# Three float32r products for the last four down projections of a dense FFN

## The reference, cut to what matters

```python
h = silu(x @ w_gate) * (x @ w_up)                 # 1024 tokens x 1024
a = abs(h.reshape(B, S, I // 4, 4))
_, idx = top_k(a, 2)                              # the two largest of each four stay
h_sparse = (g * mask).reshape(B, S, I)
return h_sparse @ w_down                          # 1024 x 256
...
x = x + tanh(g_ffn[1]) * ffn(layernorm(x))
```

## Time and profile before

| what | value |
|---|---|
| device time, 3 runs | 359.84 us median, 358.69 to 361.1 |
| profiled execution: its device time | 358.81 us |
| its span, and mean granted PE clock | 357.1 us, 0.976 |
| PE busy | 318.0 us (89%) |
| DVE busy | 258.3 us (72%) |
| ACT busy | 162.8 us (46%) |
| POOL busy | 110.3 us (31%) |

### The profile page before, as it was taken

The page is one execution under the profiler, slowest core; times in us unless marked ns, Lnnn a source line. Parts: engine busy times, 40 slices in busy tenths (PEclk is TensorE's granted clock), DMA queues, the critical chain, the costliest instruction groups (busy, mean ns, idle before and its releaser), DMA issues.

```text
span 357.1 us, 5054 instructions
## 1 busy us (share of the span) xinstructions
PE 318.0 (89%) x1630; PEld 218.0 (61%) x1639; DVE 258.3 (72%) x572; ACT 162.8 (46%) x333; POOL 110.3 (31%) x156
## 2 busy tenths in 40 slices
PE   2799886669999987999989999998979999999997
PEld 1385676547899634555544554563444886788885
DVE  4538895776677649989967996895672479999921
ACT  2333455344444222147767766775784344333000
POOL 7503575272000275501443425243554001000000
PEclk9999999658999999999999999999999999999999
DMA  6999200025311224600000000000000000000101
GB/s 190 369 418 323 51 1 16 2 88 180 101 61 59 76 59 130 284 0 9 0 7 2 1 0 9 0 3 1 6 3 0 0 2 0 2 0 0 46 30 44
DMA packets 14090, 22.96 MB, mean 64 GB/s; under 512 B 2065, under 2 KB 11409, under 8 KB 13202
## 3 DMA queue, kind: packets, MB, share of 16 engines
q1 hardware_dynamic: 13298, 20.56, 16.8%
q0 software_dynamic: 768, 2.10, 1.9%
HBM read 16.36 MB, written 6.03 MB: 63 GB/s over the span
## 4 chain that ended last, share of the span: by engine, by line
PE 61%; DVE 21%; issue 5%; ACT 4%; DMA 4%; POOL 4%; SPq 1%; DVEq 0%; ACTq 0%; POOLq 0%
PE bank L272 44%; DVE mx L1332 6%; PE bank L492 5%; PE bank L460 4%; ACT region L1008 3%; DVE stats L1078 2%; PE bank L463 2%; DMA region<-y_sorted,place 2%; PE bank L288 2%; POOL rstd L774 2%; DVE x_sb L1118 1%; DVE xn L1090 1%; PE bank L282 1%; PE bank L507 1%; POOL region L814 1%
## 5 line engine op out<-in xcount | busy, mean ns | idle before, releaser
L1008 ACT ACTIVATE region<-bank,padcol 128x512 f32<-128x512 f32 x96 | 62.3, 692 | 18.6 <-PE bank L272 17.8
L1332 DVE TENSOR_REDUCE mx<-bank 128x2 f32<-128x512 f32 (+1 forms) x96 | 60.9, 681 | 4.7 <-PE bank L463 4.1
L841 POOL TENSOR_SCALAR_AFFINE_SELECT region<-region 128x1024 f32<-128x1024 f32 x32 | 35.8, 1121 | 77.8 <-ACT region L1008 77.8
L272 PE MATMUL bank<-qst,kblk 128*128 128x512 f32 x96 | 45.7, 488 | 0.8 <-DMA qst<-nmT 0.3
L460 PE MATMUL bank<-kblk,qst 128*128 128x512 f32 x96 | 43.6, 471 | 1.7 <-DVE mx L1332 1.3
L463 PE MATMUL bank<-causb,identb 128*128 128x256 bf16 (+1 forms) x90 | 28.3, 314 | 0.0
L272 PE MATMUL bank<-e_down,region 128*128 128x256 f32 x128 | 28.0, 380 | 0.0
L1118 DVE SCALAR_TENSOR_TENSOR x_sb<-bank,tg,x_sb 128x256 f32<-128x256 f32 x24 | 11.6, 483 | 21.0 <-PE bank L272 21.0
L272 PEld LDWEIGHTS bank<-e_down,region 128*128 128x128 f32 x128 | 24.2, 190 | 3.6 <-DVE region L1481 0.3
L774 POOL TENSOR_TENSOR rstd<-veps,power 128x1 f32<-128x1 f32 x40 | 24.8, 619 | 3.3
L770 POOL TENSOR_SCALAR veps<-mv 128x1 f32<-128x1 f32 x40 | 12.8, 321 | 40.3 <-DVE mv L1080 37.5
(11 more groups left out here) (195 smaller groups left out, 737.0 us busy)
## 6 DMA issues: line engine op xcount, KB each, us to landing
e_gu<-in_e_gu_dram SPq DMA_DIRECT2D x2, 1408.0 KB, 12.2
x_sorted<-zero SPq DMA_DIRECT2D x1, 1920.0 KB, 9.4
y_sorted<-region SPq DMA_DIRECT2D x15, 128.0 KB, 1.7
x_sb<-in_x_dram SPq DMA_DIRECT2D x4, 256.0 KB, 4.1
ctxT<-in_ctxT_dram SPq DMA_DIRECT2D x2, 512.0 KB, 7.3
e_down<-in_e_down_dram SPq DMA_DIRECT2D x1, 1024.0 KB, 13.6
region<-x_sorted SPq DMA_DIRECT2D x1, 1024.0 KB, 7.4
e_gu<-in_f_gate_dram SPq DMA_DIRECT2D x1, 1024.0 KB, 6.5
```

The source lines that it names most:

```text
L272: return pe.matmul(dst, lhsT, rhs, start=first, stop=last)
L841: pool.affine_select(out=block, in_=block, compare_op=ALU.is_ge, fill=0.0, base=0, pattern=[[0, 2], [0, PER_GROUP], [1, P]], channel_multi ...
L1008: taken(act.activation(dst, src.rearrange("p (h n) -> p h n", n=SEQ - mt * P), ACT.Exp, bias=padcol[:, key:key + 1], scale=float(HD) ** -0 ...
L1332: taken(dve.reduce_max(mx[:, b % 2, nt, quads, q, hg], src, AX), "sa")
```

## The change

Four new tiles are laid over storage that is free by then: `fd_high` (in `qst`, behind the comparison results), `fd_low` (over `vaug`), `h_high` (over `kblk`) and `h_low` (over `hs[1]` itself). ACT rounds `f_down` into `fd_high` in two halves of 128x1024, behind the silu of pieces 0 and 1. POOL subtracts the two halves into `fd_low`, behind its last `inverse_std` in program order. At the end of its program ACT rounds the eight finished blocks of `hs[1]` into `h_high`, each as soon as DVE has written it, and DVE subtracts them in place into `h_low`, behind the last choice and the residual of tile 3. PE makes tiles 4 to 7 in two passes: for all four tiles the two products with `h_high` (64 matmuls), then for all four the product with `h_low` (32 matmuls). Two pairs of semaphores of earlier stages are merged into one each (`a_abs` into `a_made`, `tanh` and `vexp` into `tanh_vexp`), with the counts of their waits adapted; the order of instructions there stays.

```diff
--- before.py
+++ after.py
@@ -187,6 +187,10 @@
                   "fu": ([up_high[t][:, :] for t in range(KT)], up_low, f_up)}
 
         cmps = sb_over("cmps", [P, 6, UNIT], BF16, "qst")
+        fd_high = sb_over("fd_high", [P, FFN_MT, DIM], F32R, "qst", 2 * 6 * UNIT)
+        fd_low = sb_over("fd_low", [P, FFN_MT, DIM], F32R, "vaug")
+        h_high = sb_over("h_high", [P, FFN_MT, UNIT], F32R, "kblk")
+        h_low = sb_over("h_low", [P, FFN_MT, UNIT], F32R, "region", 4 * 6144)
         cmp1, cmp2, cmp3 = cmps[:, 0:3, :], cmps[:, 3:5, :], cmps[:, 5, :]
         wins = amat[:, :, :].rearrange("p h n -> p (h n)").bitcast(BF16).rearrange("p (c n) -> p c n", n=UNIT)
 
@@ -335,7 +339,7 @@
                 if i == 2:
                     gate(0)
                 dst = acquire(pe, "ro", i, "main")
-                pe.wait_ge(sem("a_made"), 2 * h + 2)
+                pe.wait_ge(sem("a_made"), 4 * h + 4)
                 for t in range(2):
                     ins = mm(dst, amat[:, h, t * SEQ + st * P:t * SEQ + st * P + P], v0[:, t, h, :], t == 0, t == 1)
                 ready(ins, "ro")
@@ -682,9 +686,20 @@
             pe.wait_ge(sem("hs_made"), 8)
             for k in range(UNIT_TILES):
                 down(k, "last")
-            pe.wait_ge(sem("hs_made"), 16)
+            pe.wait_ge(sem("fd_split"), 4)
             for k in range(UNIT_TILES, TILES):
-                down(k, "wide")
+                dst = acquire(pe, "res3", k, "wide")[:, 0:DIM]
+                cols = tile_cols(k % UNIT_TILES)
+                for m in range(FFN_MT):
+                    pe.wait_ge(sem("ffn_high"), 2 + m + 1)
+                    mm(dst, h_high[:, m, cols], fd_high[:, m, :], m == 0, False)
+                    mm(dst, h_high[:, m, cols], fd_low[:, m, :], False, False)
+            for k in range(UNIT_TILES, TILES):
+                cols = tile_cols(k % UNIT_TILES)
+                for m in range(FFN_MT):
+                    pe.wait_ge(sem("h_low"), m + 1)
+                    ins = mm(fills["res3", k][:, 0:DIM], h_low[:, m, cols], fd_high[:, m, :], False, m == FFN_MT - 1)
+                ready(ins, "res3")
 
 
         @block.sync
@@ -849,6 +864,12 @@
                         inverse_std(3, k, LN_EPS)
             for k in (TILES - 2, TILES - 1):
                 inverse_std(3, k, LN_EPS)
+            pool.wait_ge(sem("av1_ready"), 2 * BATCH)
+            for c in range(2):
+                ms = slice(c * FFN_MT // 2, (c + 1) * FFN_MT // 2)
+                pool.wait_ge(sem("ffn_high"), c + 1)
+                pool.tensor_tensor(out=fd_low[:, ms, :], in0=f_down[:, ms, :], in1=fd_high[:, ms, :].bitcast(F32),
+                                   op=ALU.subtract).then_inc(sem("fd_split"), 2)
 
         @block.scalar
         def _(act):
@@ -868,7 +889,7 @@
                 h, u = divmod(i, UNITS)
                 taken(act.activation(qT0[:, h, u * UNIT:(u + 1) * UNIT], filled(act, "rq", i), ACT.Copy), "rq")
             loaded(act, "gates", 3)
-            act.activation(tg[:, :], gates[:, :], ACT.Tanh).then_inc(sem("tanh"), 1)
+            act.activation(tg[:, :], gates[:, :], ACT.Tanh).then_inc(sem("tanh_vexp"), 1)
             for k in range(TILES):
                 b, t = divmod(k, 2)
                 src = filled(act, "rv", k)[:, 0:256].rearrange("p (h n) -> p h n", h=2)
@@ -904,7 +925,7 @@
 
 
             act.wait_ge(sem("routed"), 2)
-            act.activation(r_s[:, 3, :], r_s[:, 2, :], ACT.Exp).then_inc(sem("vexp"), 1)
+            act.activation(r_s[:, 3, :], r_s[:, 2, :], ACT.Exp).then_inc(sem("tanh_vexp"), 1)
 
             def projections(b):
 
@@ -1061,6 +1082,11 @@
                 if i >= 2:
                     act.wait_ge(sem("fu_taken"), i - 1)
                 taken(act.activation(silu[:, i % 2, :], src, ACT.Silu), "fg")
+                if i < 2:
+                    ms = slice(i * FFN_MT // 2, (i + 1) * FFN_MT // 2)
+                    if i == 0:
+                        loaded(act, "f", 3)
+                    act.activation(fd_high[:, ms, :], f_down[:, ms, :], ACT.Copy).then_inc(sem("ffn_high"), 1)
                 for c in range(2 * i, min(2 * i + 2, 12)):
                     finish(BATCH - 1, c)
                 if i in LATE_NORM_STEPS:
@@ -1068,6 +1094,9 @@
                 if i >= 1:
                     magnitude(i - 1)
             magnitude(4 * FFN_BLOCKS * UNITS - 1)
+            for m in range(FFN_MT):
+                act.wait_ge(sem("hs_made"), FFN_MT + m + 1)
+                act.activation(h_high[:, m, :], hs[1][:, m, :], ACT.Copy).then_inc(sem("ffn_high"), 1)
 
         @block.vector
         def _(dve):
@@ -1108,8 +1137,8 @@
                 for n, (o, w, d) in enumerate(((0, 2 * P, 0), (2 * P, P, 3 * P))):
                     dve.scalar_tensor_tensor(out=amat[:, h, d:d + w], in0=aneg[:, h, o:o + w], scalar=-1.0,
                                              in1=aneg[:, h, o:o + w], op0=ALU.mult, op1=ALU.max)\
-                       .then_inc(sem("a_abs"), 1)
-                    dve.wait_ge(sem("a_abs"), 2 * h + n + 1)
+                       .then_inc(sem("a_made"), 1)
+                    dve.wait_ge(sem("a_made"), 2 * (2 * h + n) + 1)
                     dve.tensor_scalar(amat[:, h, d:d + w], amat[:, h, d:d + w], 1.0, None, ALU.max)\
                        .then_inc(sem("a_made"), 1)
 
@@ -1145,7 +1174,7 @@
                                          op0=ALU.mult, op1=ALU.add).then_inc(sem("gn_y"), 1)
 
             loaded(dve, "gamma", 2)
-            dve.wait_ge(sem("tanh"), 1)
+            dve.wait_ge(sem("tanh_vexp"), 1)
             dve.wait_ge(sem("ro_taken"), 2)
             for k in range(2):
                 stat(4, k, o_sb[:, HALF_ORDER[k], :])
@@ -1228,7 +1257,7 @@
             step(dve.reduce_sum(slot_f[:, :], r_slot[:, :, :], AX))
             dve.tensor_scalar(slot_expert[:, :], slot_f[:, :], float(EXPERTS - 1), None, ALU.min)\
                .then_inc(sem("routed"), 1)
-            dve.wait_ge(sem("vexp"), 1)
+            dve.wait_ge(sem("tanh_vexp"), 2)
             step(dve.tensor_scalar(r_s[:, 4, :], r_s[:, 3, :], 1.0, None, ALU.add))
             step(dve.reciprocal(r_s[:, 5, :], r_s[:, 4, :]))
             step(dve.tensor_scalar(r_s[:, 11, :], r_s[:, 5, :], tg[:, 2:3], None, ALU.mult))
@@ -1503,6 +1532,10 @@
             for step in range(4):
                 sparsify(FFN_BLOCKS * UNITS - 1, step)
                 residual("res3", step, 3)
+            for m in range(FFN_MT):
+                dve.wait_ge(sem("ffn_high"), 2 + m + 1)
+                dve.tensor_tensor(out=h_low[:, m, :], in0=hs[1][:, m, :], in1=h_high[:, m, :].bitcast(F32),
+                                  op=ALU.subtract).then_inc(sem("h_low"), 1)
             for k in range(UNIT_TILES, TILES):
                 residual("res3", k, 3)
 
```

## The result

The changed kernel takes 362.16 us (median of 19 runs, 360.76 to 363.54), the kernel before 360.25 us (19 runs): a ratio of 1.0057, 95% interval 1.0041 to 1.0073. That is slower by 2.1 us (1.5 to 2.6), inside the range of the forecast and on the other side of the kernel before than the 359.4 us given.

A forecast was written before the change was run, and what follows sets the result against it. The chain ending last was taken as PE alone from 304.00 us, hanging on DVE's program at 298 to 304. -2.9 + 3.0 = +0.1 gave 358.9, or 359.9 on the runs' scale; 359.4 was given, range 356.4 to 362.6.

The forecast's parts named there:

- The gain on PE: Down projections of tiles 4 to 7: 96 float32r matmuls take 11.5 us instead of 14.1 plus 0.3 waiting, gain 2.9 us.
- The 64 waits: New waits on PE's queue ahead of each block: taken at nothing; at 0.04 us each, 2.6 us would go.
- The rival of three products that are no faster: Tail matmuls on PE: pitch stretches from 0.1175 to 0.144 us, only the delay stays, 361.8 to 362.8; chance 0.10.
- What feeds the products: ACT's h_high and DVE's h_low ready before PE asks, 0.6 and 1.6 us to spare; ACT's weight roundings cost nothing.
- The hold on DVE: Behind 299.6 us POOL's two subtractions, 2.2 us each, block DVE; tile 7's x_low and PE come 3.0 us late.
- The two instructions named: On DVE: tile 7's normalization, 1.29 us late, then the first count of wins, 1.66 us more.
- the line through 128x1 and 128x256: POOL's time for a 128x1024 subtraction, from 0.22 us for one column and 0.73 for 256: 2.26 us.
- the estimate of 2.25: POOL's 128x1024 subtraction, as half of the Trainium skill's 4497 ns for 2048 float32 columns: 2.25 us.
- The sum: Whole kernel: gain of 2.9 us against delay of 3.0 us, +0.1 on the profiled 358.81 us, so 358.9.
- the fall of the clock in them: Rival: PE's clock falls in its idle stretches of about 1.6 and 2.9 us, 361.8 to 362.8; chance 0.13.
- a sign that its sum is wrong: Stretch behind PE's start of group 2: a clock below 1.00 there would show the sum wrong.
- the two bounds: Price of a lower PE clock: 1.3 us by the later earlier-seen stretch alone, 2.9 us by both.

The follow-up runs named there:

- e1: The change, with POOL making both halves of fd_low ahead of the inverse deviations of tiles 6 and 7; 357.46 us, ratio 0.9935 to the kernel before.
- e4: The change, with 12 unused bfloat16 matmuls ahead of PE's wait for tile 7's x_low; 360.23 us, ratio 1.0023 to the kernel before.
- e3: The change, without h_high and h_low, last four tiles projected in float32, fd_high and fd_low made for nothing; 364.65 us, ratio 1.0151 to the kernel before.
- e2: The change, with one half of fd_low made early, the other still behind tile 7's inverse deviation; 358.76 us, ratio 0.9968 to the kernel before.
- e3b: A second profiled execution of e3, program unaltered; 365.95 us in one run.

## Why the prediction was right or wrong

*The gain on PE: right.* 2.9 us were forecast, from a pitch of 0.1175 and a wait of 0.31 that goes; 0.1168 was the pitch, and PE's path is 2.79 us shorter in e1, where nothing disturbs it (2.3 by the runs, 1.5 to 3.2). The 64 waits cost nothing that shows. The rival of three products that are no faster is refuted.

*What feeds the products: right.* 0.94 us to spare at the last `h_high`, 1.96 at `h_low`, ACT's roundings hidden, and 2.63 us from PE's last matmul to the end of the span.

*The hold on DVE: right in mechanism and place, a term too small.* The two instructions named were held, in the order named. POOL's half was taken at 2.2 us and takes 2.40 to 2.46 where DVE does not hold it; the line through 128x1 and 128x256, with its 2.26, was too flat, and the estimate of 2.25 beside it in the prediction is 0.2 short as well. Each hold grew by 0.2: 1.49 and 1.87 where 1.29 and 1.66 stood, 3.36 in place of 3.0. That also settles what no row before showed: a count in bfloat16 waits for POOL as well. The Trainium skill's rule (SBUF — State Buffer, section "SBUF: two separate sides") agrees in every trace here with POOL's subtraction beside DVE, also in that operations with an input in PSUM passed (`x_low` kept its 0.41 us, the multiply its 0.69).

*The sum: wrong, by the step that kept the clock out of it.* The prediction saw the holes to 0.1 us (1.6 and 2.9), named the fall of the clock in them as a rival, put it at nothing in the sum, and gave it 0.13 because PE worked densely until 300 us and again for 1.8 us between the holes. That did not prevent it: in both profiled executions of the change the clock fell in the second hole, and in the first of them the stretch of 4 us around the start of group 2 had 0.61; a clock below 1.00 there was named in the prediction as a sign that its sum is wrong. The price was 1.53 us (49.17 in the change, 47.64 in e1), between the 1.3 and the 2.9 of the two bounds, and e4, which fills the hole, gets it back. With it: 3.36 + 1.53 - 2.79 = +2.1 us, which is what the runs give. Without it, +0.6.

*The side.* The sum as worked out was +0.1; the time given, 359.4, lay below the median of before because it was set between the scale of the profiled execution and that of the runs. The profiled execution had the shorter early fall of the clock (mean clock 0.976), and the 1.0 us between those fits that; they are no part of the change. A forecast of no change should have been put on the scale of the median.

## What to carry to other kernels

Work given to POOL because it has time is not free: what counts is which DVE instruction runs into it, and who waits for that one. Look in POOL's program for the place where DVE works from PSUM; here the same 4.8 us cost 3.4 us of delay behind tile 7 and nothing 20 us earlier. And where a change leaves two holes on PE as long as those here, 1.7 and 3.0 us, count the clock into the sum, not among the mishaps.

## What was not expected of the hardware

The clock fell with no hole longer than 2.98 us, after 1.8 us of dense matmuls between two holes, and not in every execution of the same program: in one execution of e3 it stayed at 1.00, in another it fell 0.8 us after PE had begun again. Holes of 1.7 and 1.1 us, as in e2, left it at 1.00 in the execution profiled. Where it fell, it stayed low for about 3.4 us (308.9 to 312.3 in the change, 310.2 to 313.6 in e3b). What decides between the executions stays open; no run here tells it.
